# Self-attention of a decoder layer: VectorE makes banks 1, 2, 3 and 4 of the probabilities' low halves and GpSimd bank 0, where VectorE made 1 and 3 and GpSimd 0, 2 and 4

## The reference

```
q = (x @ Wq.T + bq)   # 32 heads of 32;  k, v: 16 heads of 32
scores = where(causal, q k^T * SCALE, -inf)
w   = softmax(scores, axis=-1)
out = w @ v           # query heads h and h + 16 share key/value head h
```

## Time and profile before

| | |
|---|---|
| median of 3 runs | 3142.64 us |
| span of the profiled execution | 3137.7 us, 4.9 us under the median of the runs |
| TensorE matmuls busy | 2697.5 us (86%) |
| VectorE busy | 2164.6 us (69%) |
| ScalarE busy | 1634.1 us (52%) |
| GpSimd busy | 1042.4 us (33%) |
| low halves on VectorE, L919 | 128 instructions |
| low halves on GpSimd, L381 | 192 instructions, mean 1185 ns |
| high halves on ScalarE, L744 | 320 instructions, mean 628 ns |

### The profile page before, as it was taken

How to read it: one execution, slowest core, us unless ns; L and a number is a source line. 1 busy time by engine, 2 the same in 40 slices (tenths; PEclk the granted TensorE clock), 3 DMA queues, 4 the chain that set the end, 5 groups by cost and what they waited for, 6 DMA issues and landing times.

```text
span 3137.7 us, 55227 instructions
## 1 busy us (share of the span) xinstructions
PE 2697.5 (86%) x18464; PEld 1426.6 (45%) x18464; DVE 2164.6 (69%) x3396; ACT 1634.1 (52%) x2962; POOL 1042.4 (33%) x938
## 2 busy tenths in 40 slices
PE   5987797798789637898989889898988989898899
PEld 3655555565556424343434334343433434343344
DVE  5566666757675677677676777766777776677765
ACT  3554455355346447646446464654646455464642
POOL 2333434334344433323223242322323232232422
PEclk8997897999799767999999999999999999999999
DMA  5111210211111031111111111111111111111112
GB/s 159 58 45 30 63 38 23 69 39 45 35 57 32 1 127 65 47 44 51 41 46 48 39 54 47 51 43 40 53 40 52 42 53 40 40 53 40 54 40 117
DMA packets 97817, 161.65 MB, mean 52 GB/s; under 512 B 20720, under 2 KB 39664, under 8 KB 97648
## 3 DMA queue, kind: packets, MB, share of 16 engines
q1 hardware_dynamic: 97648, 159.47, 16.2%
HBM read 123.61 MB, written 16.78 MB: 45 GB/s over the span
## 4 chain that ended last, share of the span: by engine, by line
PE 24%; issue 15%; DVE 12%; ACT 9%; POOL 1%; DMA 1%; SPq 0%; DVEq 0%; ACTq 0%; POOLq 0%
PE f_bank L1348 17%; PE f_bank L1329 6%; DVE line L1456 5%; ACT line L1371 5%; DVE line L1453 5%; ACT h L1399 1%; POOL w L1255 1%; DMA codes<-in_codes 1%; ACT hT_h L1404 1%; DVE w L1461 1%; ACT dn_h L1376 1%; ACT up_h L1376 1%; SPq L1216 0%; DVE h L1491 0%; DVE y L1497 0%
## 5 line engine op out<-in xcount | busy, mean ns | idle before, releaser
L1371 ACT ACTIVATE line<-codes 128x512 f32<-128x512 int32 x1512 | 846.8, 620 | 539.8 <-DVE line L1456 259.5
L1329 PE MATMUL f_bank<-fT_h,up_h 128*128 128x512 f16 x1792 | 681.5, 380 | 31.5 <-POOL up_l L1260 29.1
L1329 PE MATMUL f_bank<-fT_l,up_h 128*128 128x512 f16 x1792 | 681.1, 380 | 0.0
L1329 PE MATMUL f_bank<-fT_h,up_l 128*128 128x512 f16 x1792 | 681.0, 380 | 0.0
L1456 DVE TENSOR_TENSOR line<-line 128x512 f32<-128x512 f32 x840 | 618.8, 790 | 0.0
L1274 POOL TENSOR_TENSOR hT_l<-h,hT_h 128x512 f16<-128x512 f32 x112 | 147.0, 1313 | 1020.1 <-ACT hT_h L1404 1020.0
L1348 PE MATMUL f_bank<-dn_h,hT_h 128*128 128x512 f16 x896 | 349.8, 390 | 109.4 <-DVE y L1497 107.7
L1497 DVE SCALAR_TENSOR_TENSOR y<-f_bank,y 128x512 f32<-128x512 f32 x448 | 304.5, 685 | 114.5 <-PE f_bank L1348 114.3
L381 POOL TENSOR_TENSOR p_l<-p,p_h 128x512 f16<-128x512 f32 x192 | 227.6, 1185 | 432.5 <-ACT p_h L744 431.6
L1491 DVE SCALAR_TENSOR_TENSOR h<-f_bank,h 128x512 f32<-128x512 f32 x112 | 77.5, 692 | 419.0 <-ACT h L1399 276.2
L1348 PE MATMUL f_bank<-dn_l,hT_h 128*128 128x512 f16 x896 | 349.8, 390 | 0.0
(11 more groups left out here) (132 smaller groups left out, 4690.0 us busy)
## 6 DMA issues: line engine op xcount, KB each, us to landing
codes<-in_codes SPq DMA_DIRECT2D x168, 256.0 KB, 2.9
scales<-in_scales SPq DMA_DIRECT2D x336, 128.0 KB, 2.9
xn<-in_x SPq DMA_DIRECT2D x16, 512.0 KB, 3.9
x_sb<-in_w SPq DMA_DIRECT2D x16, 512.0 KB, 5.5
q_rows<-nat_h SPq DMA_DIRECT2D x256, 32.0 KB, 1.9
x_sb<-in_x SPq DMA_DIRECT2D x16, 512.0 KB, 3.8
x<-x_sb SPq DMA_DIRECT2D x16, 512.0 KB, 2.6
y<-x SPq DMA_DIRECT2D x4, 2048.0 KB, 12.0
```

The source lines that it names most:

```text
L1329: mm = nc.tensor.matmul(bank[(GATE, UP)[kind] + n % 2][:, :], w[:, chunk, kind, P * c:P * c + P], x[:, c, cols], start=(m == 0), stop=(m = ...
L1371: nc.scalar.activation(line[:, m, :], codes[:, slot, :], ACT.Copy, scale=slope, bias=intercept)\
```

## The change

The low halves of banks 2 and 4 go from GpSimd to VectorE. Wherever VectorE made bank 3's low half it now makes those of banks 2, 3 and 4, one after the other; `low_parts(b, n + 2)`, which takes `BY_VECTOR` as it stands, now makes four. GpSimd's loop makes bank 0's alone. TensorE's `weigh` waits for bank 0 (GpSimd's) and bank 4 (VectorE's) in place of 3 and 4. ScalarE's waits follow `low_cut`.

```diff
-        BY_VECTOR = (1, 3)
+        BY_VECTOR = (1, 2, 3, 4)
...
-                for k in (CHUNKS - 2, CHUNKS - 1):
+                for k in (0, CHUNKS - 1):
                     pe.wait_ge(*low_cut(b, CHUNKS * n + k))
...
                     maxima(b, n + 2 + j, (0, 1, 2))
                     low_parts(b, n + j, (1,))
                     maxima(b, n + 2 + j, (3, 4))
-                    low_parts(b, n + j, (3,))
+                    low_parts(b, n + j, (2, 3, 4))
...
                 low_parts(b, n + 3, (1,))
                 if more:
                     maxima(b, nn, (2, 3, 4))
-                low_parts(b, n + 3, (3,))
+                low_parts(b, n + 3, (2, 3, 4))
```

## The result

The changed kernel takes 3183.58 us (median of 4 runs, 3174.74 to 3189.45); the kernel before, run beside it, 3142.77. The ratio is 1.013, 95% interval 1.0108 to 1.0152: slower by 40.8 us, where 29 were forecast, 1.4 times as much. The time lies in the range given, 3152 to 3188, but near its upper end and outside the 3163 to 3180 that the forecast gave itself; the number nearest to it is the clock rival's 3182.

The account below looks back on a forecast made before the run. VectorE's queue, which TensorE awaits for maxima, was taken to bound self-attention. Terms summing to 29.05 us raise the span from 3137.7 to 3166.7; with 4.9 added, the forecast was 3172 us, range 3152 to 3188.

Parts of the forecast that it names:

- the clock rival: More waiting holds TensorE longer at its lower clock, 10 us of slower matmuls in all: 3182; chance 0.12.
- What bounds: Self-attention: VectorE's queue decides TensorE's waits for row and bank maxima; GpSimd is off the path, relieving it gives nothing.
- First halves: Added low halves: units without statistics 0.9 us, unit 2 with statistics 5.55, unit 3 6.6 plus 0.7 in the last batch.
- Second halves of units 0 to 2: Late low halves of pair 3 delay pair_out and the next unit's maxima, in 12 units: 12.6 us.
- 0.85 + 0.2 = 1.05 a unit: Second halves of units 0 to 2: 0.85 for pair 3's late low halves, 0.2 for earlier delay; between 0.75 and 1.4.
- Second halves of unit 3: Each pair's low halves end 0.45 us later in three batches, 2.7 us; nothing in the last batch.
- What was costed at nothing: TensorE's changed semaphore waits, ScalarE's exponentials waiting for low halves four banks back, and DMAs: no cost.
- The stalls: VectorE and GpSimd excluding each other: 14.2 us on low halves and 9.1 on copies, 23.3 us at most to win.
- The 4.9 us that I added to the span: Distance of the runs' median, 3142.64, above the profiled span, added to the forecast span of 3166.7 us.

Follow-up runs that it names:

- run 1: Kernel before with the low halves of banks 2 and 4 made by nobody, GpSimd making bank 0 alone: 3135.73 us, ratio 0.997.
- run 5: Changed kernel with pair 1's three low halves moved in VectorE's queue from ahead of the row maxima to just ahead of pair 2's: 3150.82 us.
- run 11: Kernel before with bank 3's low halves moved from VectorE to GpSimd, which so makes four banks of five: 3123.71 us, ratio 0.9929.
- run 9: Kernel before with pair 1's low half of bank 3 moved from ahead of the row maxima to just ahead of pair 2's low halves: 3128.9 us.
- The filler: 16 unread matmuls ahead of each mid-unit wait for row maxima: 3136.14 us on the kernel before, 3172.85 on the changed one.
- run 10: Changed kernel with pair 3's low halves of banks 2 and 4 cut to 8 columns in second halves of units 0 to 2: 3159.24 us.
- run 12: Kernel before with pair 1's bank 3 low half moved behind the row maxima, plus 8 unread matmuls ahead of pair 2's scores: 3130.27 us.

## Why the prediction was right, and where its size was off

- **The number.** The direction and the range held, and the mechanism, VectorE's queue ahead of its maxima. The forecast's own 3163 to 3180 did not: its 3172 was 11.6 us short. That the time fell so near to the clock rival's 3182 is in part luck, since that rival placed its 10 us in matmuls behind longer idling and the runs leave the size of the clock's share open.
- **What bounds.** Right. GpSimd was not on the path; its relief gave 6.7 us (run 1), and the place in VectorE's queue decides (run 5; run 11 agrees).
- **First halves.** Right, term by term: 2.0, 5.9 and 6.9 us against 0.9, 5.55 and 7.3. That the work in units 0 and 1 is hidden by a wait and a stall is seen in the rows at 96.77 and 98.73. But a move out of that place is worth much more than the change adds there: 33 us in the changed kernel (run 5) and 14 in the kernel before (run 9). I had looked at what the change adds there and not at what stood there.
- **Second halves of units 0 to 2.** The mechanism right, the size wrong: 21.8 us for 12.6. The failed step is "0.85 + 0.2 = 1.05 a unit". VectorE's side of it was right: the late three take 1.80 us, the low half behind the addition keeps its stall, and unit 0 came out at 4.3 us for 4.2. The term had nothing for TensorE taking longer over the same matmuls. In units 1 and 2 it did, by 13.4 us, at a granted clock that fell to 0.76 to 0.85. The filler, which changes nothing on VectorE, took back 9.2 us of these halves, or 6.7 when it stands in both kernels. So part of the excess hangs on the clock, and the rest stays open. Which wait lowers the clock is open too: in run 5 TensorE waited for row maxima only 8.8 us in all, and unit 2's second halves were still granted 0.83, 0.78, 0.79 and 0.93. My rival on the clock had the mechanism at 10 us and the place wrong in part: I looked at unit 3, where the clock was at or near its lower level already (0.50 to 0.58 in the second halves of the first three batches).
- **Second halves of unit 3.** Right, 2.9 for 2.7, and batch by batch: 0.9, 0.95 and 1.0 us where 0.9 was forecast, and nothing in the last batch.
- **What was costed at nothing.** ScalarE waited for GpSimd's bank 0 by 5.0 us in all (0.2 before). GpSimd's new order is not enough for it: in run 1 that order is the same and the wait is absent. It comes with the added low halves on VectorE. I had put the risk at VectorE's banks; it is small, and not separated from the rest.
- **The stalls.** The copies' 9.1 us went, in full. The Trainium skill (SBUF — State Buffer, section Who interferes with whom) says that a VectorE instruction with two SBUF inputs contends with a GpSimd instruction that reads SBUF. The low half at 215.72 agrees, 1.45 us beside a GpSimd one from 215.47 to 216.62. The relief is real, and a seventh of what the same low halves cost on VectorE.
- **Open.** The changed kernel's runs spread over 15 us, those of before beside them over 4; but the kernel before spread over 18 us in a later group, so no claim hangs on it. The 4.9 us that I added to the span should have been some 1.8, so the sum for the span was short by 9.6 us and the sum for the time by 11.6. How much of run 10's factor of 1.7 is the clock and how much a common shift of the executions isn't settled.

## What to carry to other kernels

Before moving work between engines, ask what stands at the places where the receiving engine's queue is awaited, not how busy it is: at 64% busy VectorE had no room where it mattered, and the slower engine, which was hardly awaited, was the better place. The same instructions a few places later in the queue, behind what the others wait for, gave 33 us. And where TensorE's waits in a stretch grow, look at what clock it was granted there: a sum of waits alone leaves out that the same matmuls may take longer. To see what such an effect is worth, put the remedy into both kernels and not only into the changed one.

## What the hardware showed that I had not expected

Sixteen unread matmuls of 128x256 in each of 16 waits made the kernel before faster by 0.22% (0.08 to 0.36), and the changed one by 10.7 us by the medians, with intervals that overlap. In the second halves of units 0 to 2 the time at the lower level fell from 54 to 40 us in the first and from 101 to 70 in the second. The same idea at a wait of 1.2 us on average (run 12) gave nothing.
